# Attention of the last stage: key blocks added on GpSimd before TensorE sums them

## The chip, the core and the metric

The kernel runs on one core of a Trainium2 chip. The time is device microseconds (us) of one execution. TensorE (PE in the profile) multiplies into PSUM, which has eight banks; VectorE (DVE), ScalarE (ACT) and GpSimd (POOL) do the elementwise work; SyncE (SP) issues the transfers. POOL has no way to PSUM here: all that it reads and writes in this kernel is SBUF. The engines run on their own and meet at semaphores.

## The reference

Two layers, each an attention and a feed-forward network, on 8 batches of 256 tokens of width 512. The part that the change touches is the attention of the second layer (the names are those of the reference):

```python
def attention(q, k, v):
    scale = 1.0 / jnp.sqrt(jnp.asarray(HD, q.dtype))
    scores = jnp.einsum('bqhd,bkhd->bhqk', q, k) * scale
    probs = jax.nn.softmax(scores, axis=-1)
    return jnp.einsum('bhqk,bkhd->bqhd', probs, v)
...
q = rms_norm(linear(x, q_w, q_b), norm_q_w).reshape(B, L, NH, HD)
k_img = rms_norm(linear(ctx_img, k_img_w, k_img_b), norm_k_img_w).reshape(B, -1, NH, HD)
v_img = linear(ctx_img, v_img_w, v_img_b).reshape(B, -1, NH, HD)
...
x = x + jnp.tanh(g_xattn[1]) * _L1_xattn_ref(_layernorm(x, axis=-1), ctx_2048, ...)
x = x + jnp.tanh(g_ffn[1]) * _L1_ffn_ref(_layernorm(x, axis=-1), L1_ffn_w_norm, L1_ffn_w_gv, L1_ffn_w_out)
```

NH is 16 heads of HD = 32. The context has 256 rows, all of which fall to the image part. So each head has a 256 by 256 matrix of exponentials, and the softmax divides the weighed values by the sums of those exponentials over the 256 keys.

## The kernel before

It has four parts, a to d: the first attention, the first feed-forward network, the second attention (c) and the second feed-forward network (d). All five engines' programs are written out by hand, in the order in which the instructions run; nothing is reordered later. Parts c and d are pipelined over "turns": in turn t the keys and queries of batch f = t are made, batch b = t - 1 goes through the attention, batch c = t - 2 gets its output projection, and batch d = t - 3 goes through the feed-forward network. Turns 1 and 2 are written out by themselves and have no matmuls of part d; turns 3 to 7 are a loop; turn 8 (b = 7) and the end are written out again.

Within part c the 16 heads go in four groups g of four heads j. For a group PE does `c_probs` (L757): scores with the keys on the partitions, in two blocks kb of 128 keys, into banks 0 to 3, one head a bank, and then the negative maxima added by a second set of matmuls (L768). ACT's `c_probs` (L1173) takes the exponentials into `PT`, which has room for two groups (`h % 8`). PE's `c_weigh` (L773) multiplies `PT` with the values (`what` 0) and with a matrix of ones (`what` 1), 8 matmuls each (two key blocks, four heads), 32 rows for each head, into one bank: the weighed values in its left half, the sums in its right. DVE's `c_weigh` (L1651) takes the reciprocal of the right half (L1656), multiplies (L1658) and so frees the bank. An f32 matmul shows as two in the trace, so the 8 of either kind are 16 there.

```python
for what in range(2):
    for kb in range(TB):
        for j in range(4):
            h = 4 * g + j
            lhs = keep["ones"] if what else bufW["V"][:, b % 2 * TB + kb, h * DH:(h + 1) * DH]
```

The banks 4 to 7 are shared by all that is not scores. `places.turn` (L259 to L264) is a table by hand: a row of names for each bank, in order; whoever takes a bank waits until the name before it in the row has been read. Names that matter here: `w0` to `w3` for the weighing of group 0 to 3, `xt0`, `xt1` for the turned rows of the next batch, `y0`, `y1` for the output of part d, `g0`, `v0` for the first gate and value product of a turn.

POOL's program (from L2070) holds the small inverse roots: `c_keys_root`, `c_queries_root`, `c_rstd` (of the rows of the next batch) and `d_line` (11 operations on two columns, for part d's norm). In turn 2 `d_line(0)` comes after the roots of the queries; in later turns it comes before them. DVE's `stats(f + 1)` makes the input of `c_rstd`, and its `c_norm_x(f + 1)` needs the result; PE's `c_turn_x(f + 1)` turns what `c_norm_x` made. SP loads the keys of a batch with `load_keys_of` (L375) from a scratch in HBM, into two places in turn.

Of the kernel before, what the change touches and what calls it, by code (L numbers as in the profile page):

```python
# [6 lines left out]
ALU = mybir.AluOpType  # L7
# [7 lines left out]
D = 512  # L15
# [3 lines left out]
NB = 8  # L19
# [26 lines left out]
    c_pv c_pvr c_pjq c_qss c_qinv c_qn c_qt c_qtr c_po c_xo c_const c_vb c_vo c_vor c_bias  # L46
# [106 lines left out]
def build(nc, x, ctx, ctxT, gates, w0, w1, wkv, wqo, vec, wnorm, cols, cst, masks, selq, selc, out):  # L153
    with ExitStack() as stack:
# [35 lines left out]
        bufW = area(w0f, [("K", (2 * TB, D), F32), ("KT", (2 * KD, S), F32), ("QT", (2 * KD, S), F32), ("V", (2 * TB, D), F32),  # L190
# [70 lines left out]
        for turn in range(3, NB):  # L261
            places.turn(turn, ("g0 v1 g3 pq0 v6 v7 ut0.0 y0 xt0", "v0 po1 v3 g4 v5 g7 tq1 w1 w2 w3", "po0 g2 kt0 v4 pq1 w0 qt1 ut1.1 y1",
                               "g1 v2 kt1 g5 g6 mt tq0 ut0.1 qt0 ut1.0 xt1"))
# [17 lines left out]
        def keys_of(f):  # L281
            return bufW["K"][:, f % 2 * TB:(f % 2 + 1) * TB, :] if f else bufC["K0"]
# [16 lines left out]
        def sync_program(sp):  # L299
# [75 lines left out]
            def load_keys_of(f):  # L375
                sp.wait_ge(s.st_kv0, 32 * (f + 1))
                sp.wait_ge(s.st_kv1, 32 * (f + 1))
                sp.wait_ge(s.c_kt, max(0, 2 * (f - 1)))
# [43 lines left out]
        def tensor_program(pe):  # L422
# [350 lines left out]
            def c_weigh(b, g):  # L773
# [4 lines left out]
                for what in range(2):  # L778
# [6 lines left out]
                mm.then_inc(s.c_pv, 1)  # L785

# [125 lines left out]
            for turn in range(3, NB):  # L912
                f, b, c, d = turn, turn - 1, turn - 2, turn - 3
                c_scores(b, 0)
                d_value_gate(d, 0)
# [21 lines left out]
                c_probs(b, 2)  # L937
                c_weigh(b, 1)
                d_out_product(d, 0)
                d_turn_q(c)  # L940
                c_probs(b, 3)
                c_weigh(b, 2)
                d_turn_u(d, 1)
                if f + 1 < NB:
                    c_turn_x(f + 1)
                c_weigh(b, 3)
                d_out_product(d, 1)
# [52 lines left out]
        def scalar_program(act):  # L1000
# [348 lines left out]
        def vector_program(v):  # L1349
# [538 lines left out]
            for turn in range(3, NB):  # L1888
# [262 lines left out]
```

## Time and profile before

| what | us |
|---|---|
| runs | 1139.71, 1140.21, 1144.2 (median 1140.21) |
| the profiled execution | 1139.14 |
| its span, first to last instruction | 1137.4 |
| PE busy in the span | 1096.0 (96%) |
| DVE busy | 832.7 (73%) |
| ACT busy | 567.2 (50%) |
| POOL busy | 74.5 (7%) |

Start times in the rows below are us from the start of the span. A view of instructions in order of time has start, duration, engine, line, operation and count; in brackets stands the idle time before it and what ended it. A busy time of PE of 96% doesn't say that its stream is dense: matmuls overlap, so the time of a block is read from the start of one block to the start of the next.

The batches of part c: b = 0 has its exponentials from 664 to 681, b = 1 from 703 to 722, and the turns 3 to 7 begin at 722.5, 783.4, 844.3, 904.6 and 965.1; turn 8 begins at 1025.4.

### The profile page before, as it was taken

The numbers are of one execution on the slowest core, as the hardware profiler recorded it, in microseconds if no ns is written. First come the engines' busy times: TensorE is split into PE (matmuls) and PEld (weight loads), VectorE is DVE, ScalarE is ACT, GpSimd is POOL, SyncE is SP. The second block draws the span as 40 slices with busy tenths as digits, with TensorE's granted clock in tenths as the row PEclk, the third lists the DMA queues.
The fourth block names the chain that finished last, engine by engine and source line by source line (L and its number), as shares of the span: only waits on it lengthen the run. The fifth ranks groups of instructions, "written<-read, shape, count | busy, mean of one in ns | idle before, by whom it ended". The sixth has DMA issues, their size and how long they took to land.

```text
span 1137.4 us, 25529 instructions
## 1 busy us (share of the span) xinstructions
PE 1096.0 (96%) x10342; PEld 669.3 (59%) x10450; DVE 832.7 (73%) x1440; ACT 567.2 (50%) x918; POOL 74.5 (7%) x180
## 2 busy tenths in 40 slices
PE   8899999999999999999999999899999999999998
PEld 3455555556777777777777655455454545454543
DVE  5688888788767648566565667886868778777795
ACT  3676667766433333333333452455554637372654
POOL 0000000000000000000001012010101010101010
PEclk9899999999999999999999999999999999999999
DMA  9565555443212011021010201101010100000001
GB/s 361 185 194 169 181 193 156 154 122 122 67 38 65 20 38 37 20 75 28 29 57 20 84 2 38 37 2 56 1 57 1 57 1 30 10 11 11 10 10 38
DMA packets 29268, 79.24 MB, mean 70 GB/s; under 512 B 3041, under 2 KB 3297, under 8 KB 28897
## 3 DMA queue, kind: packets, MB, share of 16 engines
q1 hardware_dynamic: 29152, 77.61, 21.0%
q8 instruction: 84, 1.38, 0.5%
q14 instruction: 32, 0.25, 0.1%
HBM read 65.02 MB, written 12.58 MB: 68 GB/s over the span
## 4 chain that ended last, share of the span: by engine, by line
PE 89%; issue 3%; ACT 3%; DVE 2%; DMA 2%; SPq 1%; POOL 0%; ACTq 0%; DVEq 0%; POOLq 0%
PE bank L587 10%; PE bank L586 10%; PE bank L692 10%; PE bank L672 9%; PE bank L545 9%; PE bank L795 8%; PE bank L425 5%; PE bank L825 5%; PE bank L783 5%; PE bank L745 3%; PE bank L764 3%; PE bank L477 2%; PE bank L498 2%; PE bank L510 2%; PE bank L450 2%
## 5 line engine op out<-in xcount | busy, mean ns | idle before, releaser
L586 PE MATMUL bank<-ARENA,W 128*128 128x256 f16 x1024 | 227.3, 273 | 0.7 <-issue 0.7
L587 PE MATMUL bank<-ARENA,W 128*128 128x256 f16 x1024 | 227.2, 273 | 0.0
L1002 ACT ACTIVATE ARENA<-bank 128x512 f32<-128x512 f32 (+3 forms) x143 | 92.9, 687 | 81.3 <-PE bank L425 32.6
L545 PE MATMUL bank<-ARENA 128*128 128x512 f32 x256 | 119.4, 609 | 1.4 <-DMA ARENA<-in_wkv 1.4
L795 PE MATMUL bank<-W,ARENA 128*128 128x512 bf16 x493 | 116.6, 382 | 2.5 <-issue 0.7
L692 PE MATMUL bank<-ARENA 128*128 128x512 f32 x256 | 116.9, 600 | 0.0
L672 PE MATMUL bank<-W,ARENA 128*128 128x512 bf16 x472 | 114.6, 379 | 2.2 <-issue 0.2
L586 PEld LDWEIGHTS bank<-ARENA,W 128*128 128x128 bf16 x1024 | 100.0, 98 | 19.5 <-issue 1.3
L587 PEld LDWEIGHTS bank<-ARENA,W 128*128 128x128 bf16 x1024 | 100.1, 98 | 17.9
L1002 ACT ACTIVATE ARENA<-ARENA 128x512 f16<-128x512 f32 x64 | 40.3, 630 | 136.1 <-DVE ARENA L1585 129.6
L1585 DVE SCALAR_TENSOR_TENSOR ARENA<-bank,ARENA 128x512 f32<-128x512 f32 x64 | 48.0, 750 | 76.4 <-PE bank L587 73.5
L1195 ACT ACTIVATE ARENA<-bank,ARENA 128x512 f32<-128x512 f32 x64 | 43.7, 685 | 112.7 <-PE bank L795 105.5
L1999 POOL TENSOR_TENSOR ARENA<-ARENA 128x2 f32<-128x2 f32 (+1 forms) x72 | 49.2, 684 | 673.0 <-DVE ARENA L1372 435.4
L795 PEld LDWEIGHTS bank<-W,ARENA 128*128 128x128 bf16 x512 | 49.0, 98 | 66.3 <-issue 11.6
L1116 ACT ACTIVATE ARENA<-bank 128x512 f32<-128x512 f32 x64 | 38.2, 596 | 91.5 <-PE bank L587 91.4
L1382 DVE TENSOR_REDUCE ARENA<-bank 128x4 f32<-128x512 f32 x64 | 58.3, 952 | 34.6 <-PE bank L450 34.4
L1625 DVE TENSOR_REDUCE ARENA<-bank 128x4 f32<-128x1024 f32 x64 | 75.2, 1218 | 9.3 <-PE bank L745 9.3
L545 PEld LDWEIGHTS bank<-ARENA 128*128 128x128 f32 x256 | 47.4, 192 | 56.4 <-issue 52.5
L672 PEld LDWEIGHTS bank<-W,ARENA 128*128 128x128 f16 x512 | 49.9, 99 | 48.8 <-issue 1.9
L1591 DVE TENSOR_TENSOR ARENA<-ARENA 128x512 f16<-128x512 f32 x64 | 44.2, 691 | 46.5 <-ACT ARENA L1002 46.5
L1656 DVE RECIPROCAL ARENA<-bank 128x256 f32<-128x256 f32 x32 | 56.2, 1756 | 29.6 <-PE bank L783 29.6
L692 PEld LDWEIGHTS bank<-ARENA 128*128 128x128 f32 x256 | 46.6, 190 | 52.6 <-issue 51.5
(179 smaller groups left out, 1766.5 us busy)
## 6 DMA issues: line engine op xcount, KB each, us to landing
W<-in_w SPq DMA_DIRECT2D x48, 512.0 KB, 4.0
ARENA<-in_w SPq DMA_DIRECT2D x24, 512.0 KB, 3.6
kv_store<-ARENA SPq DMA_DIRECT2D x32, 256.0 KB, 3.8
W<-kv_store SPq DMA_DIRECT2D x15, 512.0 KB, 4.0
ARENA<-in_ctxT SPq DMA_DIRECT2D x8, 512.0 KB, 3.8
X<-in_x SPq DMA_DIRECT2D x8, 512.0 KB, 5.8
ARENA<-in_ctx SPq DMA_DIRECT2D x8, 512.0 KB, 5.9
out<-X SPq DMA_DIRECT2D x16, 256.0 KB, 2.0
```

The costliest lines, as they stand in the source:

```text
L425: mm = pe.transpose(to[:, k * P:(k + 1) * P], tile, one)
L545: mm = pe.matmul(bank, bufA["KT"][:, b % 2 * KD + k, t * P:(t + 1) * P], W[:, k, :], start=(k == 0), stop=(k == KD - 1 and what == 1))
L586: pe.matmul(bank[:, i * S:(i + 1) * S], W0[:, at:at + P], xt_half(b, 0)[:, k, :], start=(k == 0), stop=False)
L587: mm = pe.matmul(bank[:, i * S:(i + 1) * S], W0[:, at:at + P], xt_half(b, 1)[:, k, :], start=False, stop=(k == KD - 1))
L672: mm = pe.matmul(banks[6 + t], hx(q, what)[:, i * S + t * P:i * S + (t + 1) * P], W0[:, UP_AT + m * D:UP_AT + (m + 1) * D], start=(m == 0 ...
L692: pe.matmul(to, src[:, k, t * P:(t + 1) * P], WQ[w][:, k, :], start=(k == 0), stop=False)
L783: mm = pe.matmul(part(to, j)[:, what * S:(what + 1) * S], lhs, bufC["PT"][:, h % 8, kb * S:(kb + 1) * S], start=(kb == 0), stop=True, skip ...
L795: mm = pe.matmul(to, QQ[d][:, t, k * P:(k + 1) * P], W1[:, at:at + D], start=(k == 0), stop=(k == KD - 1))
L825: mm = pe.matmul(to, UT[d, t][:, k * P:(k + 1) * P], W1[:, UP_AT + k * D:UP_AT + (k + 1) * D], start=(k == 0), stop=(k == KH - 1))
L1002: return act.activation(to, src, ACT.Copy)
L1382: got = v.tensor_reduce(NM[:, t, :, g % 2], bank[:, 0:4, t * P:t * P + (t + 1) * P], AX_X, ALU.max, negate=True)
L1625: got = v.tensor_reduce(NM[:, t, :, g], bank[:, 0:4, t * S:(t + 1) * S], AX_X, ALU.max, negate=True)
```

## The change

`c_weigh` keeps only the matmuls with the values (for b = 7 it is as before). For b = 0 to 6 POOL adds the two key blocks of `PT` of a group, 128 by 1024 elements of f32, into a new place `PS` (`c_add`), and a new `c_sum` on PE multiplies `PS` with the ones: 4 matmuls in place of 8, into the same half of the same bank. `PS` has one place: `c_add` waits for the `c_sum` before. ACT, which writes `PT` again, now waits for `c_add` too. DVE's `c_weigh` waits for `c_sum`.

`PS` takes the memory of the second place of the keys; the load of the keys of batch f waits until the keys of f - 1 have been turned. In the turns 3 to 7 the table of banks, the place of `c_turn_x`, and the order of DVE's `c_weigh(b, 1)`, `d_integers16(d, 1)` and `d_store(d, 0)` change.

```diff
@@ keys @@
-        bufW = area(w0f, [("K", (2 * TB, D), F32), ...
+        bufW = area(w0f, [("K", (TB, D), F32), ("PS", (4, S), F32), ...
-            return bufW["K"][:, f % 2 * TB:(f % 2 + 1) * TB, :] if f else bufC["K0"]
+            return bufW["K"] if f else bufC["K0"]
-                sp.wait_ge(s.c_kt, max(0, 2 * (f - 1)))
+                sp.wait_ge(s.c_kt, 2 * f if f > 1 else 0)
@@ banks of the turns 3 to 7 @@
-            places.turn(turn, ("g0 v1 g3 pq0 v6 v7 ut0.0 y0 xt0", "v0 po1 v3 g4 v5 g7 tq1 w1 w2 w3", "po0 g2 kt0 v4 pq1 w0 qt1 ut1.1 y1",
-                               "g1 v2 kt1 g5 g6 mt tq0 ut0.1 qt0 ut1.0 xt1"))
+            places.turn(turn, ("g0 v1 g3 pq0 v6 v7 ut0.0 y0 w2 y1", "v0 po1 v3 g4 v5 g7 tq1 w1 w3", "po0 g2 kt0 v4 pq1 w0 qt1 ut1.1 xt1",
+                               "g1 v2 kt1 g5 g6 mt tq0 ut0.1 qt0 ut1.0 xt0"))
@@ TensorE @@
-                for what in range(2):
+                for what in range(2 if b == NB - 1 else 1):
+            def c_sum(b, g):
+                to = bank_c(f"w{g}", b)[0]
+                pe.wait_ge(s.c_add, 4 * b + g + 1)
+                for j in range(4):
+                    mm = pe.matmul(part(to, j)[:, S:2 * S], keep["ones"], bufW["PS"][:, j, :], start=True, stop=True, skip_group_check=True)
+                mm.then_inc(s.c_sum, 1)
@@ ScalarE, c_probs @@
+                    act.wait_ge(s.c_add, max(0, min(4 * (NB - 1), 4 * b + g - 1 if g >= 2 else 4 * (b - 1) + g + 3)))
@@ VectorE, c_weigh @@
-                v.wait_ge(s.c_pv, 4 * b + g + 1)
+                v.wait_ge(s.c_sum if b < NB - 1 else s.c_pv, 4 * b + g + 1)
@@ VectorE, turns 3 to 7 @@
-                c_weigh(b, 1)
                 d_integers16(d, 1)
                 d_store(d, 0)
+                c_weigh(b, 1)
@@ GpSimd @@
+            def c_add(b, g):
+                half = bufC["PT"][:, 4 * (g % 2):4 * (g % 2) + 4, :]
+                pool.wait_ge(s.c_ex, 8 * b + 2 * g + 2)
+                pool.wait_ge(s.c_sum, 4 * b + g)
+                pool.tensor_tensor(bufW["PS"], half[:, :, 0:S], half[:, :, S:2 * S], ALU.add).then_inc(s.c_add, 1)
...
-                if f + 1 < NB:
-                    c_rstd(f + 1)
+                for g in range(NG):
+                    if g == 2 and f + 1 < NB:
+                        c_rstd(f + 1)
+                    if f - 1 < NB - 1:
+                        c_add(f - 1, g)
```

The order of PE in batch 1 (turn 2), from the weighing of its group 0 to the first product of part d. L783 is the weighing with its sums, L764 and L768 a group's scores, L425 a turn (transpose), L745 the scores of the next batch, L795 a product of part d. Before:

```order
L783 MATMUL bank<-ARENA,W 32x256 x8
L783 MATMUL bank<-ARENA 32x256 x8
L425 MATMUL bank<-ARENA 128x128 x16
L783 MATMUL bank<-ARENA,W 32x256 x8
L783 MATMUL bank<-ARENA 32x256 x8
L745 MATMUL bank<-W 128x256 x8
L795 MATMUL bank<-W,ARENA 128x512 x8
```

And after, where L791 is `c_sum` and L802 the product of part d:

```order
L783 MATMUL bank<-ARENA,W 32x256 x8
L425 MATMUL bank<-ARENA 128x128 x8
L791 MATMUL bank<-W,ARENA 32x256 x4
L425 MATMUL bank<-ARENA 128x128 x8
L783 MATMUL bank<-ARENA,W 32x256 x8
L745 MATMUL bank<-W 128x256 x8
L791 MATMUL bank<-W,ARENA 32x256 x4
L802 MATMUL bank<-W,ARENA 128x512 x8
```

The sums of group 2 moved between the turn of part d's input and the turn of the next batch's rows, those of group 3 behind the scores of the next batch.

The order of POOL in turn 2, from the start of the last inverse root of `d_line(0)` on. Before, L1999 is an inverse root, L2043 the last operation of `d_line`, L2017 the first of the next keys' root:

```order
L1999 TENSOR_TENSOR ARENA<-ARENA 128x2 [waits s_pool_own]
L2043 TENSOR_TENSOR ARENA<-ARENA 128x2 [waits s_pool_own]
L1999 TENSOR_TENSOR ARENA<-ARENA 128x2 [waits s_c_ve]
L2017 TENSOR_SCALAR ARENA<-ARENA 128x2 [waits s_c_kn,s_c_kss]
L1999 TENSOR_TENSOR ARENA<-ARENA 128x2 [waits s_pool_own]
```

And after, where L2021 is an inverse root, L2065 the last operation of `d_line` and L2081 `c_add`:

```order
L2021 TENSOR_TENSOR ARENA<-ARENA 128x2 [waits s_pool_own]
L2065 TENSOR_TENSOR ARENA<-ARENA 128x2 [waits s_pool_own]
L2081 TENSOR_TENSOR W<-ARENA 128x1024 [waits s_c_sum,s_c_ex] x2
L2021 TENSOR_TENSOR ARENA<-ARENA 128x2 [waits s_c_ve]
L2081 TENSOR_TENSOR W<-ARENA 128x1024 [waits s_c_sum,s_c_ex] x2
L2039 TENSOR_SCALAR ARENA<-ARENA 128x2 [waits s_c_kn,s_c_kss]
```

Two adds stand behind `d_line(0)`, the other two behind `c_rstd(3)`.

The order of PE in a turn of the loop, from the weighing of group 0 to the next turn; L825 (after: L832) is the output product of part d. Before:

```order
L783 MATMUL bank<-ARENA,W 32x256 x8
L783 MATMUL bank<-ARENA 32x256 x8
L425 MATMUL bank<-ARENA 128x128 x16
L764 MATMUL bank<-W 128x256 x8
L768 MATMUL bank<-ARENA 128x256 x8
L783 MATMUL bank<-ARENA,W 32x256 x8
L783 MATMUL bank<-ARENA 32x256 x8
L825 MATMUL bank<-W,ARENA 128x512 x16
L425 MATMUL bank<-ARENA 128x128 x8
```

After, the last twelve blocks of such a turn:

```order
L791 MATMUL bank<-W,ARENA 32x256 x4
L783 MATMUL bank<-ARENA,W 32x256 x8
L832 MATMUL bank<-W,ARENA 128x512 x16
L791 MATMUL bank<-W,ARENA 32x256 x4
L425 MATMUL bank<-ARENA 128x128 x8
L764 MATMUL bank<-W 128x256 x8
L768 MATMUL bank<-ARENA 128x256 x8
L783 MATMUL bank<-ARENA,W 32x256 x8
L791 MATMUL bank<-W,ARENA 32x256 x4
L425 MATMUL bank<-ARENA 128x128 x16
L783 MATMUL bank<-ARENA,W 32x256 x8
L425 MATMUL bank<-ARENA 128x128 x8
```

Behind these come half of the output product, the sums of group 3, and the other half. The sums of group 0 and 2 now stand beside a weighing, those of group 1 and 3 alone among wide matmuls.

## Rows read from the trace of the kernel before

**Rows 1.** The page: busy times, and the chain that ended last by engine.

```profile
PE 1096.0 (96%) x10342; PEld 669.3 (59%) x10450; DVE 832.7 (73%) x1440; ACT 567.2 (50%) x918; POOL 74.5 (7%) x180
...
PE 89%; issue 3%; ACT 3%; DVE 2%; DMA 2%; SPq 1%; POOL 0%; ACTq 0%; DVEq 0%; POOLq 0%
```

**Rows 2.** Turn 5 as one stretch: us, then busy us by engine, PEclk, DMA.

```profile
844.30:904.60 60.30, 59.16 (x486) 30.91 (x490) 47.49 (x81) 32.67 (x48) 6.32 (x18) 1.00 0.09 28
```

**Rows 3.** PE in turn 4 in order of time: start us, us, engine, line, operation.

```profile
823.01 1.07 PE L783 MATMUL bank<-ARENA,W 128*32 128x256 f32 x16
823.89 1.04 PE L783 MATMUL bank<-ARENA 128*32 128x256 f32 x16
824.87 1.07 PE L425 MATMUL bank<-ARENA 128*128 128x128 bf16 x16
...
829.26 3.40 PE L825 MATMUL bank<-W,ARENA 128*128 128x512 bf16 x15 [0.16 <-issue]
832.50 0.61 PE L425 MATMUL bank<-ARENA 128*128 128x128 bf16 x8
...
834.33 1.07 PE L783 MATMUL bank<-ARENA,W 128*32 128x256 f32 x16
...
838.27 0.66 PE L425 MATMUL bank<-ARENA 128*128 128x128 f32 x4 [0.56 <-ACT ARENA L1002]
```

**Rows 4.** PE in turn 7, where no rows are turned.

```profile
1020.00 1.07 PE L783 MATMUL bank<-ARENA,W 128*32 128x256 f32 x16 [1.34 <-DVE ARENA L1658]
```

**Rows 5.** The page: a two-input operation on DVE; busy us and mean ns of one.

```profile
L1591 DVE TENSOR_TENSOR ARENA<-ARENA 128x512 f16<-128x512 f32 x64 | 44.2, 691 | 46.5 <-ACT ARENA L1002 46.5
```

**Rows 6.** One line of `d_line` on POOL: ns min/median/max; and its first in time.

```profile
L2027 POOL TENSOR_SCALAR ARENA<-ARENA x8: 218/218/780, 705.0 to 1083.2; 128x2 f32<-128x2 f32 x8
```

**Rows 7.** DVE at the same moment, an operation with two SBUF inputs.

```profile
704.90 1.42 DVE L1691 SCALAR_TENSOR_TENSOR ARENA<-X,ARENA 128x512 f32<-128x512 f32 x2
```

**Rows 8.** Batch 0 and the start of turn 2, all engines in order of time.

```profile
670.04 1.94 ACT L1178 ACTIVATE ARENA<-bank 128x1024 f32<-128x1024 f32 x2
...
673.31 1.07 PE L783 MATMUL bank<-ARENA,W 128*32 128x256 f32 x16
...
675.91 0.70 POOL L1999 TENSOR_TENSOR ARENA<-ARENA 128x2 f32<-128x2 f32 x1 [10.70 <-DVE ARENA L1372]
...
677.90 0.99 DVE L1375 TENSOR_SCALAR ARENA<-X,ARENA 128x512 f32<-128x512 f32 x2
...
682.54 3.70 PE L692 MATMUL bank<-ARENA 128*128 128x512 f32 x8
...
683.73 2.35 DVE L1625 TENSOR_REDUCE ARENA<-bank 128x4 f32<-128x1024 f32 x2
...
686.39 1.15 PE L745 MATMUL bank<-W 32*128 32x256 f32 x16
```

**Rows 9.** Batch 1, PE in order of time.

```profile
707.41 1.07 PE L783 MATMUL bank<-ARENA,W 128*32 128x256 f32 x16
...
719.66 1.08 PE L425 MATMUL bank<-ARENA 128*128 128x128 f32 x8 [2.79 <-DVE ARENA L1375]
...
724.94 0.39 PE L795 MATMUL bank<-W,ARENA 128*128 128x512 bf16 x1 [0.29 <-DVE ARENA L1658]
```

**Rows 10.** Batch 1, POOL in order of time: `d_line(0)` ends, then `c_rstd(3)`.

```profile
709.52 0.19 POOL L2043 TENSOR_TENSOR ARENA<-ARENA 128x2 f32<-128x2 f32 x1
718.17 0.69 POOL L1999 TENSOR_TENSOR ARENA<-ARENA 128x2 f32<-128x2 f32 x1 [8.45 <-DVE ARENA L1372]
```

**Rows 11.** Batch 1, DVE: the reciprocal of group 0.

```profile
709.41 1.76 DVE L1656 RECIPROCAL ARENA<-bank 128x256 f32<-128x256 f32 x1 [1.78 <-PE bank L783]
```

**Rows 12.** Two stretches with the granted clock (after POOL's busy time), as in Rows 2.

```profile
28.50:38.60 10.10, 6.24 (x46) 3.46 (x47) 8.91 (x17) 7.87 (x13) 0.70 (x1) 0.50 0.52 178
702.00:722.50 20.50, 16.83 (x251) 10.41 (x249) 16.64 (x34) 12.38 (x17) 4.88 (x12) 1.00 0.01 2
```

**Rows 13.** PE in the first of those stretches.

```profile
32.36 0.40 PE L435 MATMUL bank<-ARENA 32*128 32x64 bf16 x16 [4.73 <-ACT ARENA L1002]
```

More of the change, by code:

```diff
@@ L45 @@
     c_ve c_rstd c_xn c_xt c_xtr c_kss c_kinv c_kn c_kt c_ktr c_sc c_scr c_mhl c_mt c_mtr c_st c_ex
-    c_pv c_pvr c_pjq c_qss c_qinv c_qn c_qt c_qtr c_po c_xo c_const c_vb c_vo c_vor c_bias
+    c_pv c_add c_sum c_pvr c_pjq c_qss c_qinv c_qn c_qt c_qtr c_po c_xo c_const c_vb c_vo c_vor c_bias
     d_st d_line d_hw d_xr d_tq d_q d_sv d_qt d_qtr d_g d_gu d_sg d_u d_so d_tu d_u16 d_ut d_utr d_utv d_y d_res
@@ L189, in build @@
         w0f = W0[:, :].bitcast(F32)
-        bufW = area(w0f, [("K", (2 * TB, D), F32), ("KT", (2 * KD, S), F32), ("QT", (2 * KD, S), F32), ("V", (2 * TB, D), F32),
+        bufW = area(w0f, [("K", (TB, D), F32), ("PS", (4, S), F32), ("KT", (2 * KD, S), F32), ("QT", (2 * KD, S), F32), ("V", (2 * TB, D), F32),
                           ("u", (TB, HID), F32)])
@@ L881, in tensor_program @@
             c_weigh(0, 0)
+            c_sum(0, 0)
             c_probs(0, 2)
             c_weigh(0, 1)
+            c_sum(0, 1)
             c_probs(0, 3)
@@ L886, in tensor_program @@
             c_turn_x(2)
+            c_sum(0, 2)
             c_weigh(0, 3)
             c_scores(1, 0)
+            c_sum(0, 3)
             c_project_q(2, 0)
@@ L902, in tensor_program @@
             c_weigh(1, 0)
+            c_sum(1, 0)
             c_probs(1, 2)
             c_weigh(1, 1)
+            c_sum(1, 1)
             c_probs(1, 3)
@@ L907, in tensor_program @@
             d_turn_q(0)
+            c_sum(1, 2)
             c_turn_x(3)
@@ L914, in tensor_program @@
                 c_scores(b, 0)
+                if turn == 3:
+                    c_sum(1, 3)
                 d_value_gate(d, 0)
@@ L937, in tensor_program @@
                 c_probs(b, 2)
+                c_sum(b, 0)
                 c_weigh(b, 1)
                 d_out_product(d, 0)
+                c_sum(b, 1)
                 d_turn_q(c)
@@ L942, in tensor_program @@
                 c_weigh(b, 2)
+                c_sum(b, 2)
                 d_turn_u(d, 1)
+                c_weigh(b, 3)
                 if f + 1 < NB:
                     c_turn_x(f + 1)
-                c_weigh(b, 3)
-                d_out_product(d, 1)
+                d_out_product(d, 1, 0, KH // 2)
+                c_sum(b, 3)
+                d_out_product(d, 1, KH // 2)
             b, c, d = NB - 1, NB - 2, NB - 3
```

## Prediction

> **What bounds the kernel now.** I read the page first: PE is busy 96% of the span and makes up 89% of the chain that ended last [rows 1]. Then the stretches: in a turn of the loop PE has 59.2 us of 60.3, DVE 47.5, and POOL 6.3, all at full clock [rows 2]. Then PE in order of time inside a turn: its blocks follow each other without a hole, but for one wait of 0.56 us for ACT [rows 3]. So in turns 3 to 7 a microsecond taken from PE is one taken from the time, if nothing new waits. Last I read batches 0 and 1, where part d has no matmuls yet. There PE is not dense: it waits 2.79 us for DVE in one place [rows 9], and POOL and DVE pace it. The same edit has to be priced twice, once for five dense turns and once for two thin ones.
>
> **What goes away.** A group's weighing starts at 823.01 and its sums at 823.89, so 16 instructions take 0.88 us, and the next block starts 0.98 later: 0.10 of that is the change to wide matmuls [rows 3]. Half the sums go: 0.44 us a group, 28 groups, 12.4 us at most.
>
> **What the add costs on POOL.** No row shows POOL on a large tile. DVE takes 691 ns for 512 elements with two SBUF inputs [rows 5], so 1.38 us for 1024; POOL's bounds are once and twice DVE's pace, 1.4 to 2.8 us. I take 2.3, nearer to twice, since I know of no reason that POOL should keep DVE's pace. The Trainium skill (GPSIMD Engine Reference, 3. Performance versus the Vector engine) advises against elementwise work here and measures 4497 ns for an f32 add of 2048 elements; half of that, an estimate, is 2.25 us, and the sum below would come out 0.2 us lower. No run here shows it yet.
>
> **Does the add hold up DVE?** The same POOL operation takes 218 ns seven times or so and 780 ns at 705.0 [rows 6]; at that moment DVE runs a two-input operation from SBUF [rows 7]. So the two engines do stand in each other's way. For DVE behind a POOL operation I take the bounds 0 and the whole add. The Trainium skill (SBUF, Who interferes with whom) states an exclusive lock on a shared pair of ports, held for a whole instruction by whichever began, against DVE's two-input and two-port operations; the trace agrees in the one direction that it shows. Without any lock the sum below would be 0.9 lower.
>
> **Turns 3 to 7.** PE loses 4 x 0.44 = 1.78 us a turn. The sums of groups 0 and 2 stand beside a weighing and cost no change of form; those of groups 1 and 3 stand alone and cost it twice each: 4 x 0.1 = 0.4. Are the adds hidden? Group 0's begins with the exponentials' end, about 1.3 us before the weighing, and has the weighing, a turn of 1.0 and two blocks of scores, 3.6 us in all: hidden. Group 1's begins after sum 0 and has the weighing and the output product of 16 x 0.216: hidden. Group 2's is the tight one: it begins when sum 1 is done and `c_rstd` has run, and sum 2 follows after the turn (832.50), the scores and the weighing (834.33 + 0.88), which is 2.7 us [rows 3]; less 0.2 for two semaphores, an add of up to 2.5 is hidden. Group 3's has a turn, a weighing and half the output product: hidden. Two stalls change. `y1` now waits for `w2`, and the turned rows for ACT's copies; by DVE's and ACT's order both come free within 0.3 us of PE's arrival, where PE now waits 0.28 to 0.56. And the next turn's `g0` waits for the store of `y1`, which on DVE is queued behind the later weighing of group 3: 0.25. A turn so gains 1.78 - 0.4 - 0.25 = 1.13, or 1.0 in the turns with the smaller wait before: 4.2 for four. Turn 7 has today a wait of 1.34 us for bank `w3` behind `w2` [rows 4]; the new table puts `w2` elsewhere, and the wait goes: 2.3. Sum of the five: -6.5.
>
> **Batch 0.** Here the chain is exponentials, scores, exponentials: ACT ends at 671.98, and PE's scores end 1.33 later at 673.31 [rows 8], since all four banks are in use. That chain stays, and the PE time saved for groups 0 to 2 is idle time. New: POOL runs `c_rstd(2)` (675.91, 0.70) and then add 2, 676.4 to 678.7. DVE's norm of the rows (at 677.90) is queued behind it if the lock holds, until 678.7. `c_turn_x(2)` waits for the norm, to 680.2; sum 2 ends 680.7; add 3 may begin only then, since `PS` has one place, and ends 683.1; sum 3 ends 683.6, and the projection starts at 683.9 in place of 682.54. Behind sum 3 stand DVE's weighing (2.2) and its maxima (2.35), to 688.3, for which PE's scores wait that now start at 686.39 [rows 8]. Cost +2.0; +1.1 without the lock; +0.2 with an add of 1.4.
>
> **Batch 1.** POOL ends `d_line(0)` at 709.71 [rows 10], and add 0 is queued behind it: to 712.1. Sum 0 stands in PE's stream straight behind the weighing that starts at 707.41 [rows 9], and behind sum 0 stand the scores of group 2. So PE idles for 3.8 us. DVE begins the reciprocal of group 0 at 712.8 and not at 709.41 [rows 11]. From there DVE works without a hole until `c_rstd(3)` starts, 8.76 us later (709.41 to 718.17), so at 721.6; add 2 stands behind it, 722.3 to 724.6, and PE waits for sum 2 ahead of `c_turn_x(3)`, where today it starts at 719.66. Then sum 2, the turn, the weighing and the scores (0.5 + 1.0 + 1.0 + 1.1) to 728.3, sum 3 to 728.75, and DVE's weighing of group 3, which frees the bank of `v0`, to 731.15. Today `v0` starts at 724.94 [rows 9]: +6.3. Two adds lie on this path, so the bounds of the add give +4.5 to +7.3.
>
> **The clock.** In this stretch PE would stand idle from about 719 to 724.7. After an idle time of 4.73 us [rows 13] the granted clock is seen at 0.50, 1.2 GHz in place of 2.4 [rows 12]; with today's 2.79 us it stays at 1.00 [rows 9, 12]. If it falls, the 3.0 us of PE work behind take up to twice as long. Bounds 0 and 3.4; I take 1.7.
>
> **Keys in one place.** SP now issues the keys of f after those of f - 1 are turned, in the middle of a turn; behind them in SP's queue stand the values of the same batch, which wait for the end of that turn anyway. ACT reads the keys early in the next turn, over 10 us later. Cost 0. If that cover were gone, a transfer of about 4 us a turn would show. ACT's new wait for `c_add` is for the group two before, long done: 0.
>
> **The sum.** -6.5 + 2.0 + 6.3 + 1.7 = +3.5 against the profiled execution's 1139.14, so 1142.6; its span is 1.7 below that, and the median is 1140.21, so the forecast for the median is 1143.7.
>
> **Rivals.**
> - The waits are cheap: an add of 1.4 us, no lock, no fall of the clock. Then -7.5 (the sums come early everywhere) + 0.2 + 4.5 = -2.8: 1137.4. For it: an add is simple work. Against: POOL's small operations are no faster than DVE's.
> - The front phases lose nothing and the turns also shed the waits for ACT: -7.8 in the turns alone, 1132.4. Against it stand the order of POOL, with `d_line(0)` ahead of add 0, and the 709.71 at which that ends.
> - The add is slow. It decides from 2.5 us on, the cover of sum 2. At 3.5 us each of the turns 3 to 7 loses 1.0, which leaves -1.5 of the gain; batch 1 costs 8.7, batch 0 about 2.8 with the lock, the clock up to 1.7: +11.7 or 1151.9; at 2.8 it is 1146.5 to 1148.5. For it: a tile of four strided pieces; against: nothing that the trace shows.
> - The keys come late after all: each turn waits for them up to 4 us, 1150 and more. Against it: 10 us of room.
>
> **How the numbers follow.** The forecast as written, 1141 to 1146, 0.50; cheap waits, 1137.4, 0.23; nothing lost in front, 0.07; slow add or more, above 1146, 0.18; late keys 0.02. The range for 8 in 10 goes from 1137 (the cheap end) to 1148.5 (an add of 2.8 with a full fall of the clock). A measurement of this kernel can tell about 0.5%, 5.7 us. Below 1134.5: 0.12, the second rival and part of the first; above 1145.9: 0.24, the slow add and the upper part of the forecast; between: 0.64.
>
> **What would show it.** POOL's line of the add gives its duration at once: 2.0 to 2.6 bears out the sum. In batch 1 PE should wait about 3.8 us for POOL behind the first weighing, and about 5 to 6 us before the sums of group 2; the turns 3 to 6 should be 59.3 to 59.9 us long in place of 60.4 to 60.9, and turn 7 58. The granted clock of batch 1 would be under 1.00. The prediction is wrong if the turns keep their length (a new wait at `g0`, `y1` or sum 2), or if batch 1 is no longer than today.

## The result, and the profile after

The changed kernel takes 1143.33 us (median of 11 runs, 1141.97 to 1149.16) against 1140.57 for the kernel before beside it (11 runs, 1139.31 to 1144.2): a ratio of 1.0036, 95% interval 1.0019 to 1.0052. The forecast was 1143.7, no change within 0.5%, and on the slow side. The profiled execution took 1142.36 against the 1142.6 of the sum. The same kernel, run 8 more times in a later group, had a median of 1146.2 (1142.42 to 1149.22) against 1141.09 for the kernel before, ratio 1.0048 [1.0031, 1.0064]. So the median moves by 3 us from group to group, and that the first one fell within 0.4 us of the forecast is in part chance. Both groups have the changed kernel slower, by 2.8 and 5.1 us.

The page of the changed kernel, busy times and the chain that ended last by engine:

```profile
PE 1099.0 (96%) x10226; PEld 662.0 (58%) x10226; DVE 837.6 (73%) x1440; ACT 567.5 (50%) x918; POOL 142.5 (12%) x208
...
PE 85%; DVE 4%; ACT 4%; issue 3%; DMA 2%; POOL 1%; SPq 1%; ACTq 0%; DVEq 0%; POOLq 0%
```

Against [rows 1] PE has fewer instructions and yet is busy 3.0 us longer: some of them ran at half clock (below). POOL's busy time went up by 68.0 us, and DVE's by 4.9, though the change gives DVE nothing to do: some of its operations last longer (below). POOL and DVE have gained a share of the chain.

The line of the add on GpSimd, with its durations (min/median/max, ns), then POOL's wait for PE ahead of it, and last PE's wait for it (us, times):

```profile
L2081 POOL TENSOR_TENSOR W<-ARENA x28: 2337/2364/2385, 668.5 to 1024.1; 128x1024 f32<-128x1024 f32 x28
...
  PE bank L791: 22.6, 9
...
  PE bank L791: 8.6, 3
```

The add takes 2.36 us, nearly constant; 2.3 was taken. PE waits long for it in three places, 8.6 us in all, and each of them is in batch 0 or 1 (shown below). It is 1.71 times the 1.38 us of DVE's pace [rows 5]. The Trainium skill (GPSIMD Engine Reference, 3. Performance versus the Vector engine) gives 4497 ns for 2048 elements; the estimate of 2.25 us from it is 5% under the row.

Where the time went. A stretch here runs from the first scores of one turn to those of the next (L745), in us; "start" is all before the first scores of turn 1, "tail" all after the first scores of turn 8.

| stretch | before | after | difference |
|---|---|---|---|
| start | 645.53 | 645.34 | -0.19 |
| turn 1 (most of batch 0) | 35.93 | 36.16 | +0.23 |
| turn 2 (batch 1) | 41.07 | 50.42 | +9.35 |
| turn 3 | 60.90 | 61.27 | +0.37 |
| turn 4 | 60.84 | 59.76 | -1.08 |
| turn 5 | 60.29 | 59.19 | -1.10 |
| turn 6 | 60.57 | 59.47 | -1.10 |
| turn 7 | 60.29 | 58.40 | -1.89 |
| tail | 111.93 | 110.57 | -1.36 |

The delay of a batch doesn't end at the first scores of the next turn, so batches 0 and 1 are better read at the points of the forecast. To the second scores of turn 2 (686.39 before [rows 8], 688.74 after, and the start was 0.19 earlier) it is 2.35 + 0.19 = +2.54. From there to `v0` of turn 3 (724.94 [rows 9], 736.03) +8.74. The rest of turn 3 is -1.34, and with turns 4 to 7 that makes -6.51. Sum with start and tail: +3.2, the difference of the spans (1137.36 and 1140.57). The parts that the forecast priced come to +4.8 (2.54 + 8.74 - 6.51), where it wrote +3.5; start and tail, -1.55 together, bring the sum back to it.

Turn 5 of the changed kernel as one stretch, as [rows 2]:

```profile
852.95:912.14 59.19, 58.56 (x456) 29.77 (x455) 47.75 (x82) 32.82 (x48) 16.23 (x22) 1.00 0.09 28
```

PE is 0.6 us less busy than before, and POOL's 16.2 us lie beside it. In the turns the adds stay hidden, that of group 2 just so: in turn 5 it ends at 904.04 and its sums start at 904.17.

Batch 0 of the changed kernel, PE, DVE and POOL in order of time (start us, us, engine, line, operation):

```profile
676.26 2.37 POOL L2081 TENSOR_TENSOR W<-ARENA 128x1024 f32<-128x1024 f32 x1
...
677.57 1.78 DVE L1397 TENSOR_SCALAR ARENA<-X,ARENA 128x512 f32<-128x512 f32 x2
...
680.88 2.36 POOL L2081 TENSOR_TENSOR W<-ARENA 128x1024 f32<-128x1024 f32 x1 [2.26 <-PE bank L791]
...
683.29 0.64 PE L791 MATMUL bank<-W,ARENA 128*32 128x256 f32 x8 [0.65 <-POOL W L2081]
...
688.74 1.15 PE L745 MATMUL bank<-W 32*128 32x256 f32 x16 [0.96 <-DVE ARENA L1647]
```

The forecast's steps are all there: add 2 from 676.3, DVE's norm held (1.78 us for what took 0.99 [rows 8]), add 3 only after sum 2, sum 3 until 683.9, and the next scores at 688.7 (688.3 was written).

Batch 1 of the changed kernel, PE in order of time:

```profile
709.78 1.07 PE L783 MATMUL bank<-ARENA,W 128*32 128x256 f32 x16
714.41 0.64 PE L791 MATMUL bank<-W,ARENA 128*32 128x256 f32 x8 [3.56 <-POOL W L2081]
...
727.13 1.08 PE L791 MATMUL bank<-W,ARENA 128*32 128x256 f32 x8 [4.37 <-POOL W L2081]
728.15 1.97 PE L425 MATMUL bank<-ARENA 128*128 128x128 f32 x8
730.05 1.94 PE L783 MATMUL bank<-ARENA,W 128*32 128x256 f32 x16
...
736.03 1.04 PE L802 MATMUL bank<-W,ARENA 128*128 128x512 bf16 x4 [1.37 <-DVE ARENA L1680]
```

POOL in the same time, and one operation of DVE:

```profile
711.87 0.20 POOL L2065 TENSOR_TENSOR ARENA<-ARENA 128x2 f32<-128x2 f32 x1
712.02 2.34 POOL L2081 TENSOR_TENSOR W<-ARENA 128x1024 f32<-128x1024 f32 x1
...
724.07 0.70 POOL L2021 TENSOR_TENSOR ARENA<-ARENA 128x2 f32<-128x2 f32 x1 [6.50 <-DVE ARENA L1394]
724.74 2.34 POOL L2081 TENSOR_TENSOR W<-ARENA 128x1024 f32<-128x1024 f32 x1
...
724.88 2.93 DVE L1397 TENSOR_SCALAR ARENA<-X,ARENA 128x512 f32<-128x512 f32 x2 [0.89 <-POOL ARENA L2021]
```

Both waits of the forecast stand where it put them. Add 0 begins as `d_line(0)` ends (712.0), and PE, done with its weighing at 710.8, waits until 714.4. Add 2 stands behind `c_rstd(3)` and ends at 727.1, where PE waits 4.37 us. DVE's norm (L1397, 0.99 us [rows 8]) is held by the add and takes 2.93.

The clock in this batch (columns as [rows 12]):

```profile
715.00:718.40 3.40, 3.40 (x40) 2.10 (x40) 3.11 (x7) 0.78 (x1) 2.35 (x1) 0.50 0.00 0
...
725.30:732.10 6.80, 4.96 (x36) 2.56 (x40) 4.70 (x4) 2.51 (x4) 4.14 (x2) 0.50 0.00 0
```

It falls to 0.50 (1.2 GHz) at 715.0, 0.6 us after the first wait ended, and again at 725.3, 2.5 us into the second; before, it stayed at 1.00 here [rows 12]. The turned rows at 728.15 take 1.97 us where they took 1.08 [rows 9].

### The profile page after: what moved, and what is told of

Its sections match the earlier page's. It is cut to its first block, busy times and chain, and to the rows that moved or that the text cites. A ratio compares the mean times of both kernels' runs of the same rounds, so it can differ in the third digit from the quotient of the medians.

```text
span 1140.6 us, 25250 instructions
## 1 busy us (share of the span) xinstructions
PE 1099.0 (96%) x10226; PEld 662.0 (58%) x10226; DVE 837.6 (73%) x1440; ACT 567.5 (50%) x918; POOL 142.5 (12%) x208
## 3 DMA queue, kind: packets, MB, share of 16 engines
q8 instruction: 83, 1.36, 0.5%
## 4 chain that ended last, share of the span: by engine, by line
PE 85%; DVE 4%; ACT 4%; issue 3%; DMA 2%; POOL 1%; SPq 1%; ACTq 0%; DVEq 0%; POOLq 0%
PE bank L587 10%; PE bank L586 10%; PE bank L672 10%; PE bank L692 9%; PE bank L545 9%; PE bank L802 8%; PE bank L425 5%; PE bank L832 4%; PE bank L764 2%; PE bank L745 2%; PE bank L477 2%; PE bank L783 2%; PE bank L510 2%; PE bank L498 2%; PE bank L450 2%
## 5 line engine op out<-in xcount | busy, mean ns | idle before, releaser
L2021 POOL TENSOR_TENSOR ARENA<-ARENA 128x2 f32<-128x2 f32 (+1 forms) x72 | 51.3, 713 | 610.5 <-DVE ARENA L1394 372.9
L672 PE MATMUL bank<-W,ARENA 128*128 128x512 bf16 x512 | 120.8, 379 | 0.0
L802 PE MATMUL bank<-W,ARENA 128*128 128x512 bf16 x512 | 117.9, 379 | 2.7 <-DVE ARENA L1680 1.4
L802 PEld LDWEIGHTS bank<-W,ARENA 128*128 128x128 bf16 x512 | 48.7, 98 | 67.4 <-issue 11.1
```

The source lines that it names most:

```text
L672: mm = pe.matmul(banks[6 + t], hx(q, what)[:, i * S + t * P:i * S + (t + 1) * P], W0[:, UP_AT + m * D:UP_AT + (m + 1) * D], start=(m == 0 ...
L802: mm = pe.matmul(to, QQ[d][:, t, k * P:(k + 1) * P], W1[:, at:at + D], start=(k == 0), stop=(k == KD - 1))
L2021: return pool.tensor_tensor(to, src, keep["minus_half"][:, 0:n], ALU.pow)
```

## Experiments

Line numbers shift by some lines in kernels with additions. All were profiled, and the kernel before ran beside each: 1140.47, 1141.09 and 1141.04 us in the three groups.

**The turns alone.** In `ADDED` stand the batches that get the add; the others keep their 8 matmuls of sums. The waits that count adds and sums are changed to match; the cut below leaves them out.

```diff
+ADDED = (2, 3, 4, 5, 6)
-                for what in range(2 if b == NB - 1 else 1):
+                for what in range(1 if b in ADDED else 2):
@@ c_sum @@
+                if b not in ADDED:
+                    return
@@ GpSimd @@
-                    if f - 1 < NB - 1:
+                    if f - 1 in ADDED:
```

> The add on GpSimd and the separate sums for batches 2 to 6 alone; batches 0 and 1 sum on TensorE as in the kernel before. Theory (the change gains in the dense turns and loses in the two thin batches): the turns 3 to 7 are 1.1, 1.1, 1.1, 1.1 and 1.9 us shorter than before, batches 0 and 1 as before, so 6.5 us faster than before (up to 8 if the clock does not fall near the end), no fall of the granted clock between 700 and 740, and runs that agree within 2 us. Rival (the loss comes from something that the whole change has, the keys in one place or the table of banks): under 3 us faster than before, with waits left in turns 1 to 3.

Measured: 1134.27 us (6 runs, 1131.43 to 1138.62), ratio 0.9945 [0.9925, 0.9964]. The turns 3 to 7 are 59.58, 59.76, 59.19, 59.47 and 58.41. The same kernel run again, in another group:

> The add for b = 2 to 6 alone, again, beside the one with extra matmuls: 1134 to 1135 by both, a stretch of turn 2 of 42.7 us where the clock falls once in it and 41.1 where it does not, turns 3 to 7 of 59.6, 59.8, 59.2, 59.5 and 58.4.

Measured: 1136.03 (6 runs, 1134.11 to 1137.28), ratio 0.9948 [0.9932, 0.9965]; turns 59.63, 59.77, 59.19, 59.47, 58.41, turn 2 42.46 with one fall of the clock. So the turns give what was written, and the loss is all in front. Two things that were expected of the first run failed: its trace has a fall of the clock at 720.4, where none was written for 700 to 740, and its runs lie 7 us apart, not 2. The fall is taken up in the last experiment.

**The turns and batch 0.** `ADDED = (0, 2, 3, 4, 5, 6)`.

> As the changed kernel but for batch 1, which sums on TensorE as before. Theory: batch 0 costs 2.5 us by itself, so 2.5 us slower than the run with batches 2 to 6 alone and 4 us faster than before; no fall of the clock, since the idle times over 3 us are both in batch 1. Rival (batch 0's delay is swallowed by slack later): the same time as with batches 2 to 6 alone.

Measured: 1135.82 (4 runs, 1134.1 to 1137.26), ratio 0.9957 [0.9942, 0.9972]. Against the turns alone, the stretches of turns 1 and 2 are 0.25 and 2.33 us longer: 2.6 by the trace, 1.6 by the medians; 2.0 was written in the forecast and 2.5 for this run. Batch 1's cost follows as the rest: turns 2 and 3 are 5.36 and 1.73 longer in the changed kernel than here, and this trace has a fall of the clock in turn 2 that alone costs 1.66 (42.73 where it falls against 41.07): 8.75 in all. That fall wasn't expected here either.

**Everything but the add.** `ADDED = ()`: the new table of banks, the new orders and the keys in one place, with all 16 instructions of sums for each group.

> The table of banks, the order of the turns and the keys in one place from the changed kernel, but no add and no separate sums: every group has its 16 matmuls as before. Theory: of the turns' gain only the waits belong to the table, 1.3 us in turn 7 and up to 0.3 in each of the others, so 1 to 2.5 us faster than before. Rival (the gain in the turns is the table's and not that of fewer matmuls): 5 us or more faster.

Measured: 1136.25 (6 runs, 1135.23 to 1138.8), ratio 0.9965 [0.9952, 0.9978]; turns 60.44, 60.10, 59.82, 60.10, 58.91. Of the 6.5 us that the turns gain, 3.52 (0.46, 0.74, 0.47, 0.47, 1.38) come without any add. Only 3.0 (0.86, 0.34, 0.63, 0.63, 0.50, against the turns alone) are left for the fewer matmuls. By the runs the add is worth little: in the same group the medians are 1136.25 without it and 1134.27 with it, and their intervals overlap; the 3.0 us rest on the stretches. That is not the division that was written; the expected 1 to 2.5 us and its rival's 5 or more were both missed. The end of turn 5 shows why. Here PE in this kernel:

```profile
884.59 1.07 PE L788 MATMUL bank<-ARENA,W 128*32 128x256 f32 x16
886.46 1.07 PE L430 MATMUL bank<-ARENA 128*128 128x128 bf16 x16
...
900.64 1.09 PE L430 MATMUL bank<-ARENA 128*128 128x128 f32 x8
...
905.12 1.15 PE L750 MATMUL bank<-W 32*128 32x256 f32 x16
```

In the kernel before, the same turn has this:

```profile
898.53 0.66 PE L425 MATMUL bank<-ARENA 128*128 128x128 f32 x4 [0.28 <-ACT ARENA L1002]
```

From the first weighing to the next scores it is 20.53 us; before, the same blocks take 21.02. The last turned rows (L430) now come behind group 3's weighing and find their bank and their rows ready, where PE waited 0.28 us for ACT before: that gives 0.25. The weighing and sums of group 3 now stand ahead of f32 matmuls and not of wide ones and take 1.86 in place of 2.10: that gives the other 0.24. In turn 4, where the wait was 0.56 [rows 3], the gain is 0.74. The changed kernel in the same place:

```profile
892.48 1.07 PE L783 MATMUL bank<-ARENA,W 128*32 128x256 f32 x16
893.48 1.07 PE L425 MATMUL bank<-ARENA 128*128 128x128 bf16 x16
...
900.86 0.64 PE L791 MATMUL bank<-W,ARENA 128*32 128x256 f32 x8
901.43 0.62 PE L425 MATMUL bank<-ARENA 128*128 128x128 bf16 x8
...
906.71 1.36 PE L425 MATMUL bank<-ARENA 128*128 128x128 f32 x8
...
909.73 0.64 PE L791 MATMUL bank<-W,ARENA 128*32 128x256 f32 x8
910.31 1.90 PE L832 MATMUL bank<-W,ARENA 128*128 128x512 bf16 x8
912.14 1.15 PE L745 MATMUL bank<-W 32*128 32x256 f32 x16
913.46 1.89 PE L802 MATMUL bank<-W,ARENA 128*128 128x512 bf16 x8 [0.18 <-DVE X L1791]
```

That is 19.66 us, 0.87 less than without the add, where 4 x 0.44 = 1.78 was taken away. Weighing and sums of group 0 took 1.87 (884.59 to 886.46); the weighing alone now takes 1.00 (892.48 to 893.48). But the sums that come back on their own take 0.57 where they stand among other forms (900.86 to 901.43, 909.73 to 910.31), and what is beside them gets longer too. From the turned rows to the next scores it is 4.48 without the add (900.64 to 905.12) and 5.43 with it (906.71 to 912.14), of which the sums are 0.58: of the other 0.37, 0.32 is the output product, cut in two by the sums, and 0.05 the turned rows. Setting the sums apart costs 0.9 us a turn, not 0.4. Of the 0.87, another 0.24 goes at the end, where `g0` waits for the store of `y1` (0.18 of idle time; without the add there is none): 0.63 is left of a turn's gain. That wait was put at 0.25.

**The add twice.** The turns alone, with each add run twice in a row (4.75 us for both).

```diff
-                pool.tensor_tensor(bufW["PS"], half[:, :, 0:S], half[:, :, S:2 * S], ALU.add).then_inc(s.c_add, 1)
+                pool.tensor_tensor(bufW["PS"], half[:, :, 0:S], half[:, :, S:2 * S], ALU.add).then_inc(*own.up())
+                pool.wait_ge(*own.now())
+                pool.tensor_tensor(bufW["PS"], half[:, :, 0:S], half[:, :, S:2 * S], ALU.add).then_inc(s.c_add, 1)
```

> Batches 2 to 6 alone with the add, each add run twice, 4.7 us in place of 2.36. Theory (2.5 us of cover for the add of group 2, about 4.4 for the others): each of the turns 3 to 7 is 2.2 to 3 us longer than with one add, 11 to 15 us in all, and TensorE waits for GpSimd before the sums of group 2. Rival (there is more cover than the reckoning found): under 1 us a turn.

Measured: 1183.3 us (one run). The turns are 69.72, 69.03, 68.49, 68.60 and 66.22 long, 45.6 us more in all than with one add: a miss, by three times and more. PE in turn 5, where it waits:

```profile
912.10 0.64 PE L798 MATMUL bank<-W,ARENA 128*32 128x256 f32 x8 [0.66 <-POOL W L2090]
...
914.84 0.40 PE L430 MATMUL bank<-ARENA 128*128 128x128 bf16 x4 [1.78 <-DVE ARENA L1687]
...
922.43 1.08 PE L798 MATMUL bank<-W,ARENA 128*32 128x256 f32 x8 [2.11 <-POOL W L2090]
```

DVE in the same place, and the clock:

```profile
904.35 2.00 DVE L1700 TENSOR_SCALAR ARENA<-ARENA 128x2 f32<-128x2 f32 x1
...
906.79 3.04 DVE L1743 TENSOR_SCALAR ARENA<-ARENA 128x512 f32<-128x512 f32 x2
909.76 2.90 DVE L1747 TENSOR_SCALAR ARENA<-ARENA 128x512 bf16<-128x512 f32 x2
```

```profile
915.75:926.00 10.25, 6.92 (x68) 3.44 (x64) 9.44 (x13) 3.49 (x5) 8.07 (x4) 0.50 0.01 2
```

The wait for POOL before sum 2 is 2.11, about what the cover of 2.5 says. But DVE's operations are held (3.04 and 2.90 for what takes 0.88 and 0.76), DVE gets late for PE's banks, and the clock is at 0.50 for 10 us of the turn. The three waits shown and one of 1.22 us for DVE (918.38) come to 5.8 of the turn's 9.3 us; the other 3.5 lie in the work at half clock, which no run took apart from the waits. The forecast's rival of a slow add had only the first of the three causes in its turns; what a turn loses at the 3.5 us that it priced wasn't run. In the changed kernel the turns stand close to that edge: 2.36 against a cover of 2.5.

**Fewer columns in the add.** The add takes the first 128 of each head's 256 queries, and the sums are made from those for both halves. The sums of the second half of the queries are so left out, and the first half's stand in their place. The add has half the elements; all else is the changed kernel.

```diff
-pool.tensor_tensor(bufW["PS"], half[:, :, 0:S], half[:, :, S:2 * S], ALU.add)
+pool.tensor_tensor(bufW["PS"][:, :, 0:P], half[:, :, 0:P], half[:, :, S:S + P], ALU.add)
-mm = pe.matmul(part(to, j)[:, S:2 * S], keep["ones"], bufW["PS"][:, j, :], ...
+mm = pe.matmul(part(to, j)[:, S:2 * S].rearrange("p (a b) -> p a b", a=2), keep["ones"], doubled(bufW["PS"][:, j, 0:P]), ...
```

> The changed kernel with an add of half the columns (128 of 256 queries; the sums of the other half repeat the first, so that half of the output is divided by the wrong sums). Theory (the add is on the path once in batch 0 and twice in batch 1, and hidden in the turns): the add takes 1.2 us, batch 0 is 1.2 shorter, batch 1 2.3 to 3 shorter, turns 3 to 7 the same: 3.5 to 4.5 us faster than the changed kernel at the same clock. Rival (the order of the queues, not the add's length, makes the waits): under 1.5 us.

Measured: 1138.37 (10 runs, 1136.88 to 1143.58), ratio 0.9979 [0.9967, 0.9991]. That is 7.8 below the changed kernel's median in the same group (1146.2), and 4.4 by the spans of the two traces, whose mean clocks are 0.993 and 0.992 (1140.6 and 1136.2); 3.5 to 4.5 at the same clock was expected. The difference of the medians has falls of the clock in it. POOL's add in batch 1:

```profile
710.14 1.26 POOL L2081 TENSOR_TENSOR W<-ARENA 128x512 f32<-128x512 f32 x1
```

Turns 4 to 7 keep their length to 0.01 us (59.75, 59.19, 59.47, 58.41), so none of the add is on the path there. Batch 0 ends 1.78 earlier (the second scores of turn 2 at 686.85 against 688.74, less 0.11 for the start) and batch 1 takes 2.47 less. With 1.1 us off each add that is two adds on either path, as the forecast's working has it, the second of batch 0 in part (this run's expectation had one there). PE still waits 2.48 and 3.29 us for POOL in batch 1, 1.1 less in either place than with the whole add. An add of no length would leave some 1.4 and 2.2 us, an estimate from these two lengths: that part of the waits is POOL's order and what comes ahead of it.

**POOL's queue.** Add 0 of turn 2 ahead of `d_line(0)`.

```diff
                 if c == 0:
+                    c_add(f - 1, 0)
                     d_line(c)
-                for g in range(NG):
+                for g in range(1 if c == 0 else 0, NG):
```

> The changed kernel with the add of group 0 of batch 1 ahead of d_line(0) in GpSimd's order. Theory: the wait of 3.56 us ahead of the first sums goes, the reckoned start of the second add stays (d_line ends at 715.2 either way), VectorE's inputs and with them c_rstd(3) come 2.0 us earlier, and the first fall of the clock goes: 2 to 3.5 us faster than the changed kernel, the second idle time and its fall stay. Rival (d_line is only moved and delays as much as before): the same time.

Measured: 1143.68 (10 runs, 1140.75 to 1149.12), ratio 1.0026 [1.0011, 1.0040], beside 1146.2 for the changed kernel in the same group. The 2.5 us between the medians lie in the expected 2 to 3.5, but the traces don't bear out the reason: turn 2 is 49.30 long against 50.14, so 0.8 us is the order's and the rest isn't placed, and the clock still falls twice, at 716.9 and 727.1. The trace shows what became of the first wait:

```profile
711.43 0.64 PE L791 MATMUL bank<-W,ARENA 128*32 128x256 f32 x8
...
717.66 1.08 PE L791 MATMUL bank<-W,ARENA 128*32 128x256 f32 x8 [2.94 <-POOL W L2081]
```

```profile
715.42 2.20 DVE L1726 TENSOR_TENSOR ARENA<-ARENA 128x2 f32<-128x2 f32 x1 [1.06 <-POOL ARENA L2065]
```

The wait before sum 0 is gone and turns up before sum 1, since `d_line(0)` now stands ahead of add 1. The add that begins right behind `d_line(0)` holds up a DVE operation on two columns, which takes 2.2 us, and DVE needs its result at once. Either place of `d_line(0)` puts it ahead of an add that PE waits for; no order with it behind all the adds was tried.

**The clock in the waits.** The changed kernel, with 28 and 36 extra matmuls ahead of the sums of groups 0 and 2 of batch 1, into the half of the bank that the sums write over (`c_fill`'s last number counts fours).

```diff
+            c_fill(1, 0, 7)
             c_sum(1, 0)
@@ @@
+            c_fill(1, 2, 9)
             c_sum(1, 2)
```

Beside it ran the changed kernel again.

> The changed kernel again, to stand beside the next three on one chip. Theory (the clock falls in batch 1's idle times, for a time that differs from run to run): 2 to 9 us slower than before, with spread runs whose mean granted clock is lower where the time is longer.

> The changed kernel with work added for TensorE and nothing taken away: 28 matmuls ahead of the sums of group 0 of batch 1 (3.1 us) and 36 ahead of those of group 2 (4.0 us), into the half bank that the sums overwrite. Theory (the fall of the clock costs time of its own behind the idle time): the granted clock stays 1.00 from 700 to 740, the time is 2 to 3 us below the changed kernel's quickest runs, and the spread of 7 us goes to under 2. Rival (the clock costs nothing, since the engines wait for GpSimd and VectorE anyway): the same time or up to 0.5 us more, with the same spread.

Measured: the changed kernel 1146.2 (8 runs, 1142.42 to 1149.22), ratio 1.0048 [1.0031, 1.0064]; with the extra matmuls 1141.42 (12 runs, 1139.27 to 1144.36), ratio 1.0000 [0.9989, 1.0011]. PE in batch 1, with the extra matmuls:

```profile
722.64 0.40 PE L425 MATMUL bank<-ARENA 128*128 128x128 bf16 x4 [1.24 <-DVE ARENA L1688]
722.97 4.09 PE L791 MATMUL bank<-ARENA 128*32 128x256 f32 x72
727.43 0.64 PE L797 MATMUL bank<-W,ARENA 128*32 128x256 f32 x8 [0.37 <-POOL W L2089]
...
734.08 1.04 PE L808 MATMUL bank<-W,ARENA 128*128 128x512 bf16 x4 [1.37 <-DVE ARENA L1688]
```

The clock stays at 1.00. From sum 2 to `v0` it is now 6.65 us, where the changed kernel needs 8.90 (727.13 to 736.03): the second fall costs 2.25. The first costs nothing, since sum 2 starts no earlier without it (727.43 in place of 727.13, with everything 0.22 later from the start on); DVE, which works without a hole from 715.1 to 724.0 in the changed kernel, sets that time, and at full clock PE waits 1.24 us for it in the turned rows of part d's input (L425). The medians are 4.8 apart, more than the 2.25, and the spread of the runs stayed wide (5.1 us), where under 2 was expected: there are other falls. The repeated kernel's trace has two in the tail, which is 113.71 long, against 110.57 with none. The quickest runs, 1139.27 and 1142.42, are 3.15 apart, where 2 to 3 was expected.

**The best of both.** The turns alone, and 24 extra matmuls ahead of `c_turn_x(3)`, where PE waits 2.79 us for DVE even before the change [rows 9].

```diff
+            def c_fill(f, n):
+                to, sem, value = bank_c("xt0", f)
+                pe.wait_ge(sem, value)
+                for _ in range(n):
+                    for j in range(4):
+                        pe.matmul(part(to, j)[:, S:2 * S], keep["ones"], bufC["PT"][:, j, 0:S], start=True, stop=True, skip_group_check=True)
+            c_fill(3, 6)
             c_turn_x(3)
```

> The add for b = 2 to 6 alone (batches 0, 1 and 7 with their sums as before), and 24 extra matmuls of PE (ones with exponentials that are there, 0.44 us for four, 2.65 us) in batch 1 ahead of the turn of the next rows, into the bank that this turn writes over. There PE waits 2.79 us for DVE, and the clock stood at 0.50 for 3.4 us right behind. Theory (the idle time lets the clock fall, and the work behind it runs at half speed): the wait shrinks to about 0.1, no fall between 715 and 730, the stretch of turn 2 is 41.0 to 41.3 us in place of 42.7, and the time is 1.6 to 1.8 us below the same kernel without the extra matmuls: 1132 to 1133. Rival (the fall comes from elsewhere, from a thin stretch as a whole): the fall stays and the time is that of the kernel without them. Both: turns 3 to 7 as in that kernel.

Measured: 1133.73 (5 runs, 1132.1 to 1134.36), ratio 0.9928 [0.9911, 0.9944], against 1136.03 without the extra ones in the same group. Turn 2 is 41.10 long, as expected; the time is not in the expected 1132 to 1133, since the kernel without the extra matmuls was slower in this group too. PE there without the extra matmuls, and then with them:

```profile
720.25 1.08 PE L430 MATMUL bank<-ARENA 128*128 128x128 f32 x8 [2.79 <-DVE ARENA L1404]
721.26 1.58 PE L788 MATMUL bank<-ARENA,W 128*32 128x256 f32 x16
722.60 1.95 PE L788 MATMUL bank<-ARENA 128*32 128x256 f32 x16
```

```profile
716.50 2.80 PE L797 MATMUL bank<-ARENA 128*32 128x256 f32 x48
719.36 1.08 PE L430 MATMUL bank<-ARENA 128*128 128x128 f32 x8
720.38 1.07 PE L788 MATMUL bank<-ARENA,W 128*32 128x256 f32 x16
```

The weighing and its sums take 3.2 us behind the idle time and 1.9 behind the busy one, for the same work. This is the fastest kernel here, 7 us under the one before in the same group. A part of what it has over the turns alone (2.3 by the medians, 1.4 in this stretch) is a fall of the clock in the tail that the other trace has and this one lacks; that this comes with the extra matmuls wasn't shown.

## Why the prediction held, and where it didn't

**The price of the add** (2.3 us): 2.36. Right.

**The lock.** Right in the direction that rows of before didn't show: DVE's norm takes 1.78 and 2.93 in place of 0.99. The Trainium skill (SBUF, Who interferes with whom) says so, that the one that began keeps the shared pair of ports for its whole instruction, and the trace agrees, down to 2.20 us for an operation on two columns (L1726) that takes 0.15 when no add runs.

**Batch 0** (+2.0): +2.54, and 2.6 by adding that batch alone (1.6 by the medians). Sum 3 and the scores behind it stand within 0.5 us of the written times. Half of the difference is the 0.26 from DVE's maxima (to 688.48) to PE's scores, which the reckoning left out.

**Batch 1 and the clock** (+6.3 and +1.7): +8.74. Without any fall of the clock it is 6.5 (8.74 less 2.25), and the fall is 2.25, inside its bounds of 0 and 3.4 (the 3.0 us of work that the text names would have given 3.0 at most). Waits of 3.56 and 4.37 stand where 3.8 and 5 to 6 were written. The second is shorter for a reason that the forecast left out: PE reaches it at 722.8, and that is, counted from the end of the first wait, about 1.5 us later than written. That is not the half clock: at full clock PE waits 1.24 us for DVE just ahead of it and gets there at the same time (722.97, with everything 0.22 later). The end of the wait is DVE's and POOL's, as written.

**Turns 3 to 7** (-6.5): -6.51, but this is the step that was wrong inside. The forecast said that the fewer matmuls give 1.13 a turn, with 0.4 for setting the sums apart, and that the stalls at the turned rows and `y1` stay about as they are. The runs show 0.6 a turn for the matmuls, since setting them apart costs 0.9, and 0.5 to 0.7 a turn for the new table and order, half of it or more the wait for ACT that goes, the rest the place of group 3's weighing. Table, order and keys weren't run one by one. Turn 7's wait of 1.34 for `w3` [rows 4] went as written (1.38 without any add). The written split was 1.34 for the table (turn 7's wait) and 5.2 for the matmuls; the measured one is 3.5 and 3.0. Two terms were mis-sized by 2.2 us each, with opposite signs: this part came out right by chance.

**Keys in one place** (0): turns of the same length in all kernels that have it, and no wait for a load in them. Right.

**The tail** (0): -1.36. It has nothing of the change in it: the profile of before has a fall of the clock from 1117.3 to 1120.7, that of after none; a trace of the changed kernel with two falls is 3.1 us longer there. It is chance which of them a profile shows.

**The whole.** The priced parts come to +4.8 and not +3.5: batch 0 is 0.5 and batch 1 with the clock 0.7 over. That the profiled execution is within 0.3 us of the sum comes from the tail, where the profile of before happens to have a fall and that of after none. The mechanism stands, small gains in the dense turns and a larger loss in front; the close fit is luck.

**The rivals.** The slow add, weighed at 0.18, was nearer than its price suggested: from 2.36 to 2.5 is little, and beyond it a turn loses 9 us at 4.75, where 2.2 to 3 was expected. Cheap waits were refuted by each of their three parts: add, lock and clock. Nothing lost in front was refuted by the 11.3 us of batches 0 and 1, though its second half was right, that the turns shed the wait for ACT. Late keys didn't show.

## What to carry to other kernels

A change that pays where one engine is dense can lose it all where the same work is paced by others; price each stretch by itself and apply it only where it pays, here to five of seven batches. Work moved to a slower engine costs nothing while it has cover, and far more than its own time once it hasn't, since here it held up DVE's operations and made PE wait, and PE's clock fell. When a diff moves instructions and also removes some, run the move alone: half of the gain was the move.

## What the runs showed of the hardware

- A GpSimd add of 128 by 1024 f32 (four pieces of 256, both inputs in SBUF) takes 2.34 to 2.39 us (median 2.364), and 1.26 to 1.28 (1.271) with half the elements: from these two, an estimate of 0.18 us fixed and 2.13 ns for each element of a row.
- It holds up some DVE operations, small ones too: one with two SBUF inputs of two columns (L1726) took 2.20 us and a scalar operation on two columns (L1700) 2.00, where the same lines take 0.15 and 0.17 when no add runs. Others that began inside an add kept their time in the changed kernel: reciprocals of PSUM 1.75 us (four, such as at 902.26; 1.76 otherwise), products with one input in PSUM (L1680) 0.42, reductions (L1719) 0.68, statistics (L1387) 0.68.
- A wait of PE of 2.79 us was followed by a fall of the clock in five traces of four kernels (the turns alone, twice; with batch 0; everything but the add; the add twice) and not in that of the kernel before, with the same instructions around it. Nothing that these traces show tells which it will be. Runs of one kernel lie up to 7 us apart, the slower ones with the lower mean clock: of the changed kernel's eleven, six with a mean clock of 0.993 lie from 1142.0 to 1143.3, and five at 0.988 or 0.985 from 1146.4 to 1149.2.
- Matmuls whose results are written over, put into a wait, kept the clock at 1.00 in all three places where they were tried, and what stood behind the wait started at most 0.1 us later for them.
